# Delta sublayer: the join of the triangular inverse moved next to the next unit's first doubling, and the key copy moved behind the corner copy

## The reference, cut to what matters

```python
def step(S, inp):
    qt, kt, vt, at, bt = inp
    err = jnp.einsum('bhvk,bhk->bhv', S, kt) - vt
    S = at[..., None, None] * S - bt[..., None, None] * err[..., None] * kt[:, :, None, :]
    o = jnp.einsum('bhvk,bhk->bhv', S, qt)
    return (S, o)
...
q = _silu(_dwconv_causal(x @ Wq, conv_q_w, conv_q_b))   # k and v likewise
...
o = (o - mu) * jax.lax.rsqrt(var + 1e-05) * ln_w + ln_b
g = jax.nn.sigmoid(x @ Wg).reshape(B, T, H, DV)
return (o * g).reshape(B, T, H * DV) @ Wo
```

## Time and profile before

| | |
|---|---|
| median of 3 runs | 3354.06 us (3353.66 to 3354.33) |
| profiled execution, time | 3349.63 us |
| profiled execution, span | 3347.8 us |
| PE busy | 3202.3 us (96%) |
| DVE busy | 2408.9 us (72%) |
| ACT busy | 1946.7 us (58%) |
| POOL busy | 820.8 us (25%) |
| granted PE clock, mean | 0.99 |

### The profile page before, as it was taken

The page is one execution under the profiler, slowest core; times in us unless marked ns, Lnnn a source line. Parts: engine busy times, 40 slices in busy tenths (PEclk is TensorE's granted clock), DMA queues, the critical chain, the costliest instruction groups (busy, mean ns, idle before and its releaser), DMA issues. The chain is left out here.

```text
span 3347.8 us, 89254 instructions
## 1 busy us (share of the span) xinstructions
PE 3202.3 (96%) x34218; PEld 2635.2 (79%) x34218; DVE 2408.9 (72%) x7923; ACT 1946.7 (58%) x4769; POOL 820.8 (25%) x828
## 2 busy tenths in 40 slices
PE   6999989999999999999999969999889999999999
PEld 5888878888888888888888848888667777777787
DVE  4777778777788777788777637777666777777764
ACT  3555556666666666666666626565455555555553
POOL 2333322222222222222222323333210111111100
PEclk9999999999999999999999989999999999999999
DMA  6000000000000000000000040000000000000000
GB/s 241 1 1 1 1 8 27 21 21 17 17 18 25 18 25 18 15 21 21 21 22 18 12 162 1 1 1 1 1 1 1 2 1 1 1 5 5 5 8 10
DMA packets 51338, 66.84 MB, mean 20 GB/s; under 512 B 4962, under 2 KB 40291, under 8 KB 49379
## 3 DMA queue, kind: packets, MB, share of 16 engines
q1 hardware_dynamic: 50914, 61.13, 5.7%
HBM read 58.56 MB, written 2.56 MB: 18 GB/s over the span
## 5 line engine op out<-in xcount | busy, mean ns | idle before, releaser
L1404 DVE SCALAR_TENSOR_TENSOR d_acc<-d_raw,d_taps,d_acc 128x255 f32<-128x255 f32 x1116 | 627.4, 603 | 127.7 <-ACT d_raw L1392 114.5
L2482 ACT ACTIVATE s_probs<-s_probs,s_nmax 128x128 f32<-128x128 f32 (+1 forms) x768 | 287.0, 446 | 176.9 <-DVE s_nmax L203 176.2
L1659 ACT COPY d_power<-bank 128x768 f32<-128x768 f32 x320 | 259.0, 810 | 216.3 <-PE bank L1652 216.3
L203 DVE CUSTOM_DVE_ANT_0 s_probs<-bank,mask 128x128 f32<-128x128 f32 (+1 forms) x768 | 225.5, 349 | 108.0 <-PE bank L2463 107.9
L746 POOL TENSOR_TENSOR a_q<-a_rope 64x512 f32<-64x512 f32 x128 | 164.8, 1288 | 533.7 <-DVE a_recip L814 314.0
L1390 ACT ACTIVATE d_acc<-bank,d_tap_bias,d_taps 128x256 f32<-128x256 f32 x372 | 189.9, 561 | 162.9 <-PE bank L1368 156.4
L783 ACT ACTIVATE a_area<-a_area,a_nmax 128x128 f32<-128x128 f32 (+1 forms) x512 | 226.4, 443 | 85.7 <-DVE a_nmax L203 84.9
L203 DVE CUSTOM_DVE_ANT_0 a_area<-bank,mask 128x128 f32<-128x128 f32 (+1 forms) x512 | 159.0, 355 | 133.3 <-PE bank L764 130.8
L809 ACT COPY a_area<-bank 128x512 f32<-128x512 f32 (+1 forms) x260 | 137.2, 580 | 117.4 <-PE bank L800 117.4
L736 DVE TENSOR_TENSOR a_rope<-bank,a_sinT 32x512 f32<-32x512 f32 x256 | 177.4, 693 | 5.6
L1804 POOL TENSOR_TENSOR d_o_rs<-d_o_var,minus_half 128x4 f32<-128x4 f32 x64 | 69.6, 1087 | 402.3 <-DVE d_o_var L1798 402.3
(11 more groups left out here) (287 smaller groups left out, 8621.7 us busy)
## 6 DMA issues: line engine op xcount, KB each, us to landing
d_alpha<-d_alpha_rows SPq DMA_DIRECT2D x64, 256.0 KB, 3.6
d_g_decay<-d_running_rows SPq DMA_DIRECT2D x32, 258.0 KB, 3.5
a_w_o<-in_a_w_o SPq DMA_DIRECT2D x2, 2048.0 KB, 16.8
a_area<-in_a_q_nope SPq DMA_DIRECT2D x2, 1536.0 KB, 8.2
x<-in_x SPq DMA_DIRECT2D x8, 256.0 KB, 16.8
d_wk<-in_d_wk SPq DMA_DIRECT2D x1, 2048.0 KB
d_wq<-in_d_wq SPq DMA_DIRECT2D x1, 2048.0 KB
d_wv<-in_d_wv SPq DMA_DIRECT2D x1, 2048.0 KB
```

Of the source, the lines that this page charges most:

```text
L203: return core.nc.vector.tensor_tensor_reduce(out=out, in0=scores, in1=core.mask[:, blocks], scale=-1.0, scalar=HIGHEST, op0=ALU.add, op1=A ...
L1404: last = nc.vector.scalar_tensor_tensor(out=convolved(G, r)[:, j, d:T], in0=raw[:, r % 2, j, 0:T - d], scalar=taps[:, r // 2, h, 3 - d:4 - ...
L1659: nc.scalar.copy(power[:], b_step[:, :, 0:3 * P]).then_inc(g.step_out, 1)
L2482: last = nc.scalar.activation(own, own, ACT.Exp, scale=-1.0, bias=nmax[:, s % 2, t, i:i + 1])
```

## The change

The product of the join goes to banks 4 and 5 (`b_join`) instead of 2 and 3. It stands behind the output product and `xnT_pe`, directly ahead of the next unit's step 0. Step 0 no longer waits for the join's copy of the unit before but for its corner copy (`STEPS * u - 1`), and the join waits for the former users of its new banks: `y_ready`, `oT_affine` and, in odd units, `rhs_ready`. On ACT `xnT_act` stands ahead of `join_act`, and `k_act` stands behind `corner_act` instead of ahead of `step_act(5)`.

```diff
-        b_step = core.banks[:, 2:4]
+        b_step, b_join = core.banks[:, 2:4], core.banks[:, 4:6]
...
-            need(pe, g.step_out, STEPS * u + l)
+            need(pe, g.step_out, STEPS * u + l if l > 0 else STEPS * u - 1)
...
             pe.wait_ge(g.step_out, STEPS * u + LEVELS + 1)
+            need(pe, g.y_ready, u)
+            need(pe, g.oT_affine, u)
+            need(pe, g.rhs_ready, (u + 1) // 2 if u % 2 == 1 else 0)
             for j in range(GH):
...
-                last = nc.tensor.matmul(b_step[half(0), c, cols], corner[half(c), 0, cols],
+                last = nc.tensor.matmul(b_join[half(0), c, cols], corner[half(c), 0, cols],
...
-            nc.scalar.copy(heads, b_step[half(0), :, 0:P].rearrange("p s (q t) -> p s q t", q=2))\
+            nc.scalar.copy(heads, b_join[half(0), :, 0:P].rearrange("p s (q t) -> p s q t", q=2))\
...
                     if q is not None:
                         project_pe(pe, q + 3)
-                    if live:
-                        join_pe(pe, u)
                     if e >= 0:
                         out_pe(pe, e)
                     if n == CHUNKS - 3 and u + 3 < UNITS:
                         xnT_pe(pe, u // CHUNKS + 1, q + 4)
+                    if live:
+                        join_pe(pe, u)
...
                     if live:
-                        if not odd:
-                            k_act(act, u)
                         step_act(act, u, 5)
...
                     if live:
                         corner_act(act, u)
+                        if not odd:
+                            k_act(act, u)
                     if q is not None:
                         evacuate_act(act, q + 3)
+                    if n == CHUNKS - 3 and u + 3 < UNITS:
+                        xnT_act(act, u // CHUNKS + 1, q + 4)
                     if live:
                         join_act(act, u)
-                    if n == CHUNKS - 3 and u + 3 < UNITS:
-                        xnT_act(act, u // CHUNKS + 1, q + 4)
```

## The result

The changed kernel takes 3333.35 us (median of four runs, 3329.28 to 3339.10), the kernel before 3353.86 us (median of four, 3353.56 to 3354.33). The ratio is 0.9941, with a 95% interval of 0.9925 to 0.9957: faster by 0.6%, where 0.73% was forecast. The profiled execution took 3329.28 us against 3349.63, 20.4 us less, where the sum said 24.5. It can be read from the first and the last start of the output product, on the same tile of both kernels.

What follows compares the result with a forecast made beforehand. PE, busy 96% of the span, was taken as the bound. Terms -14.3 - 18.3 + 3.6 + 5.5 - 1.0 gave -24.5 us, from 3354.1 to about 3329.5 us (-0.73%), range 3318 to 3343.

Steps and rivals of the forecast that it cites:

- Key copy: Even units: with `k_act` behind the corner copy, PE's corner product no longer waits for ACT's level 5 copy; 0.46 us each, -14.3.
- Join's place: PE, 61 units: projection and output product adjoin, join directly precedes step 0, saving change-overs; 0.30 us each, -18.3 us.
- y behind the join's copy: Only step 0 now covers the copy `y_pe` needs: 0.95 us against 1.27 of cover, so no cost.
- Output product behind `og`: Even units: the output product comes earlier and waits for POOL's `og`; 0.12 us in 30 units, +3.6 us.
- State product behind `yw`: PE gets faster, DVE's chain does not: stalls of 0.44 us at n = 5 and 0.30 at n = 7, +5.5.
- Ends of the loop: After unit 0, step 0 runs ahead of the wait for the join's copy: -1.0 us; nothing changes outside the loop.
- No new waits: Rival: `og` and `yw` come in time because DVE and POOL also run faster; 3320.5 us, chance 0.15.
- Tile change costs: Rival: join to step 0 costs too, 0.20 us a unit saved, or the corner's wait only shrinks; 3333 to 3338, chance 0.17.
- Larger give-back: Rival: y waits 0.1 to 0.2 us a unit for the join's copy; 3339 us, 3345 without any reserve, chance 0.13.
- Slower: Rival: `y_pe` waits long in every unit because ACT reaches the join's copy late; about 3369 us, chance 0.06.
- Nothing moves: Rival: PE's gaps are only moved elsewhere; 3350 to 3357 us, chance 0.04.

Runs made afterwards that it cites:

- key copy alone: Kernel before with only `k_act` moved behind `corner_act`, the join left in its old place and banks: 3344.67 us, ratio 0.9966.
- join alone: Changed kernel with `k_act` back ahead of `step_act(5)`, so only the join's new place and banks remain: 3339.71 us, ratio 0.9952.
- `yw` first: Changed kernel with DVE's `yw` put ahead of the taps of round 3 in odd units: 3327.82 us, ratio 0.9916.
- `og` in halves: Changed kernel with `og` made in two POOL operations of two heads each, the output product waiting for the second only at its third head: 3327.44 us, ratio 0.9920.
- both: Changed kernel with `yw` ahead of the taps of round 3 and `og` made in two operations of two heads: 3320.32 us, ratio 0.9899.
- the repeat: The changed kernel measured again without any edit: 3333.28 us beside the kernel before at 3355.51, ratio 0.9934.

## Why the prediction was right

The units can be priced one by one, from the start of a y product to that of the next (us, read from the traces; the units of a kind agree within some 0.02):

| kernel | n = 1, 3 | n = 2, 4, 0 | n = 5 | n = 7 | last two together |
|---|---|---|---|---|---|
| before | 22.32 | 22.32 | 22.75 | 22.31 | 31.3 |
| key copy alone | 22.32 | 21.86 | 23.25 | 22.57 | 31.3 |
| join alone | 22.00 | 22.14 | 22.53 | 22.00 | 32.5 |
| changed | 22.00 | 21.75 | 23.06 | 22.37 | 32.5 |
| `yw` first | 22.00 | 21.75 | 22.43 | 22.06 | 32.5 |
| `og` in halves | 22.00 | 21.54 | 23.06 | 22.50 | 31.5 |
| both | 22.00 | 21.54 | 22.43 | 22.20 | 31.4 |

(A unit n = 6 holds the transposes for the next sequence and changes as the other even ones do.)

- **Key copy, -14.3.** Right in mechanism and price: the corner's start moved by 0.46, an even unit with the key copy alone is shorter by 0.46, and no wait was left. The copy behind the corner cost nothing.
- **Join's place, -18.3.** Right. An odd unit has lost 0.09 at the end of the projection, 0.10 at the start of the output product and 0.13 in the join and step 0 together (0.38 + 0.99 = 1.37 before, 1.25 after), 0.32 in all where 0.30 was said. New banks in the old place gave none of it, so it is the join's neighbours. The Trainium skill's rule (TensorEngine Tiling (Array Packing), Tiling Modes), that only a change of the mode drains TensorE, agrees with the one boundary that no row before could show: join and step 0 interleave.
- **y behind the join's copy, 0.** Right in the steady units. With nothing to cover it the hand-over costs 0.75 a unit.
- **Output product behind `og`, +3.6.** Right in mechanism, too small: 0.21 to 0.22 a unit and not 0.12, 6.3 to 6.6 in 30 units. The term that failed is POOL's duration. I took 1.37 us from the even unit of the earlier trace rows, and for the order before that was right: between 560 and 1890 us the even units have 1.37 to 1.39. In the changed kernel they have 1.45 to 1.48, as the odd ones had all along, and the median of all is:

```profile
L1836 POOL TENSOR_TENSOR d_og<-d_oT,d_gT x64: 1264/1470/1482, 537.8 to 1926.3; 128x512 f32<-128x512 f32 x64
```

  The join alone leaves 1.36 to 1.39 in even units, and there a unit loses 0.14; the key copy alone gives 1.45 to 1.47. So it is the key copy's move that made `og` slower. The section on the hardware shows why.
- **State product behind `yw`, +5.5.** The right units and nearly the size: 6.6 when taken away. PE stalls 0.63 at n = 5 and 0.31 at n = 7, where 0.44 and 0.30 were said. Two errors offset each other in part, which was luck. `og` held PE back 0.10 more, which leaves less to stall for, and DVE's way was longer, from its normalisation of o to `yw` 16.32 instead of 16.05 at n = 5 and 15.66 instead of 15.52 at n = 7. At n = 5 0.13 of it arises where `og` runs and 0.14 where the silu of round 2 runs, at n = 7 all of it at `og`.
- **Ends of the loop, -1.0.** Right at the start: from the first join to the y product it is 1.91 instead of 2.99. The y product does wait for the join's copy there, 0.60 us, once. For the last two units I had no term: they take 1.3 longer. They have no projections, so a chain PE, ACT, PE sets the time, and the join's copy now stands in it.
- **Sum.** 24.5 forecast, 20.4 measured in the profiled pair, 20.5 between the medians, 22.2 in the set of runs with the repeat. Against the forecast `og` took 2.7 more, `yw` 1.1, the last two units 1.3, and 0.06 in each unit n = 7, which stays when `yw` is first, 0.4; the join's extra 0.02 a unit is worth 1.2 the other way. That is 4.3 of the 4.1 us. The give-back was 14.6 us where 9.1 was forecast.
- **Rivals.** No new waits: refuted, both came. Tile change costs: refuted by the 0.32, though the median alone, 3333.35, would have suited its 3333 to 3338 as well as the forecast. Larger give-back: the give-back was larger, but not at y, which it named, and not by enough for its 3339. Slower: seen only when the banks were put back. Nothing moves: refuted.

## What to carry to other kernels

When PE is the bound, count its change-overs between full and quarter tiles: putting two blocks of one kind side by side was worth 0.3 us a unit here, and the price can be read from the kernel before by cutting a timeline inside a block. Then list, for every product that comes earlier, how long before it its operand is ready; what a unit gains beyond such a margin is given back, and the next order change (here `yw` ahead of the taps, `og` in halves) pays the rest. The duration of an operation on POOL or DVE is not a constant of that operation: here it depended on what the other did meanwhile, so a margin of 0.1 us between them is no margin.

## What the runs showed of the hardware

**POOL and DVE shut each other out.** A DVE product of 4 columns went from 0.16 to 1.20 us while a POOL product of 512 columns ran, and back to 0.16 when that was moved. The Trainium skill (GPSIMD Engine Reference, Specifications) says that GpSimd's SBUF interfaces are shared with VectorE, with contention for DVE instructions that have two SBUF inputs; the trace agrees, for this product and the taps have two. How large the effect is, 0.8 to 1.0 us for each such meeting, is the measurement's. Between 560 and 1890 us of the kernel before, each of the 707 tap instructions without a POOL operation beside it takes under 0.49, and 147 of the 352 with one take 1.24 to 1.51; the other 205 take no longer than without.

It goes the other way too, and that is the 1.37 and 1.47 of `og`. The tap instruction that was running when `og` was started, and `og`, in the changed kernel (n = 4; for the kernel before see the earlier trace rows):

```profile
1140.83 0.48 DVE L1404 SCALAR_TENSOR_TENSOR d_acc<-d_raw,d_taps,d_acc 128x255 f32<-128x255 f32 x1
...
1140.97 1.47 POOL L1836 TENSOR_TENSOR d_og<-d_oT,d_gT 128x512 f32<-128x512 f32 x1 [3.16 <-ACT d_oT L1828]
```

```profile
1515.69 0.48 DVE L1404 SCALAR_TENSOR_TENSOR d_acc<-d_raw,d_taps,d_acc 128x255 f32<-128x255 f32 x1
```

The tap instruction ends 0.34 us into `og` in the changed kernel and 0.25 us into it before. The listed length of `og` less this rest is 1.13 to 1.14 us in both, and 1.12 to 1.14 in every unit between 560 and 1890 us of these two kernels and of the two that hold one part of the change. So in these rows the instruction that started first ends, and the other one then takes its own time.

**The granted clock outside the loop differs from run to run.** The same changed kernel, in a window with the loop and one around a quiet place behind it, its first profiled execution and then the second (columns as in the earlier trace rows):

```profile
500.00:1920.00 1420.00, 1403.95 (x21936) 1204.73 (x21937) 1118.99 (x3095) 924.68 (x1723) 410.42 (x324) 1.00 0.08 20
...
2380.00:2440.00 60.00, 37.02 (x274) 25.65 (x272) 31.73 (x133) 26.47 (x79) 9.01 (x11) 0.86 0.00 1
```

```profile
500.00:1920.00 1420.00, 1404.37 (x21940) 1205.13 (x21940) 1118.94 (x3094) 924.32 (x1723) 410.39 (x324) 1.00 0.08 20
...
2380.00:2440.00 60.00, 37.92 (x235) 26.60 (x233) 29.45 (x119) 23.37 (x70) 8.81 (x11) 0.77 0.00 1
```

In the loop both have the full 2.4 GHz. At 2380 to 2440, where PE is busy for only some 37 of 60 us, the mean grant is 0.86 in one and 0.77 in the other, which means a longer part at 1.2 GHz. Another quiet place, 1920 to 1970, goes the other way, 0.62 and 0.66. The second execution took 3.7 us more in all and had the same loop; behind its last output product it took 1400.9 us, the first 1396.8. The first profiled execution of the kernel before has 1396.0 there, and all other traced kernels, with the same code behind the loop, 1399.1 to 1401.0. Whether the clock accounts for the whole spread was not settled.
